# Loads that wait for W_hh, and an output product from fp16 pairs that POOL splits

## The reference, cut to what matters

```python
def _L0_cond_ref(initial_state, inputs, W_ih, W_hh, b_ih, b_hh):   # B 4, T 256, D 256
    def cell(h, x):
        gi = x @ W_ih + b_ih
        gh = h @ W_hh + b_hh
        i_r, i_z, i_n = jnp.split(gi, 3, axis=-1)
        h_r, h_z, h_n = jnp.split(gh, 3, axis=-1)
        r, z = jax.nn.sigmoid(i_r + h_r), jax.nn.sigmoid(i_z + h_z)
        n = jnp.tanh(i_n + r * h_n)
        h_new = (1.0 - z) * n + z * h
        return (h_new, h_new)
...
def _L0_cond2_ref(x, emb, W_emb, b_emb, g_norm, W_qkv, g_q, g_k, W_out):
    scale, shift = jnp.split(emb @ W_emb + b_emb, 2, axis=-1)
    xn = _rms_norm(x, g_norm) * (1.0 + scale) + shift
    q, k, v = ...            # of xn @ W_qkv, 16 heads of 16
    attn = jax.nn.softmax(einsum(_rms_norm(q, g_q), _rms_norm(k, g_k)) * d ** (-0.5))
    o = einsum(attn, v)
    return o + o @ W_out
...
x = x + _L0_attn_ref(_L0_cond_ref(cond_2048, x, ...), ...)
x = x + _L0_ffn_ref(_L0_cond2_ref(x, cond_2048[:, None, :], ...), ...)
```

## Time and profile before

| | us |
|---|---|
| median of 3 runs | 997.29 |
| lowest and highest | 996.51, 998.18 |
| the profiled execution's own time | 998.43 |
| span of its profile | 996.6 |
| PE busy | 937.3 (94% of the span) |
| DVE, ACT, POOL busy | 695.4, 595.1, 582.2 |

### The profile page before, as it was taken

One profiled execution on the slowest core, in us unless ns is written; L12 is line 12 of the kernel. 1 busy time (PEld: TensorE's weight loads), 2 busy tenths in 40 slices (PEclk: granted clock), 3 DMA queues, 4 the chain that ended last, 5 costly groups with the idle time before them and its releaser, 6 DMA issues. The chain is left out here.

```text
span 996.6 us, 37702 instructions
## 1 busy us (share of the span) xinstructions
PE 937.3 (94%) x14997; PEld 755.2 (76%) x14997; DVE 695.4 (70%) x2756; ACT 595.1 (60%) x2053; POOL 582.2 (58%) x1274
## 2 busy tenths in 40 slices
PE   4899999999999999998999999878899999999997
PEld 4889999999999999987888888744455566656564
DVE  6887777777777777776666667778882856656665
ACT  4666666666666666666777777767875432332332
POOL 2577766666666666666677765368302655555652
PEclk7555555555555555557999999999999999999999
DMA  8211111111111011112222231010000143333331
GB/s 345 74 22 18 25 24 25 21 19 25 25 25 24 15 25 25 25 25 86 71 76 87 75 129 41 20 42 1 2 2 1 64 117 129 112 111 122 118 130 44
DMA packets 80474, 58.98 MB, mean 59 GB/s; under 512 B 64918, under 2 KB 71576, under 8 KB 79788
## 3 DMA queue, kind: packets, MB, share of 16 engines
q1 hardware_dynamic: 79108, 56.43, 19.6%
q10 hardware_dynamic: 1192, 0.15, 0.1%
HBM read 47.33 MB, written 8.98 MB: 56 GB/s over the span
## 5 line engine op out<-in xcount | busy, mean ns | idle before, releaser
L589 POOL COPY gp<-hq 128x16 f16<-128x16 f16 x256 | 68.2, 266 | 152.4 <-DVE hq L554 152.4
L2008 PE MATMUL gu<-wq_part 128*128 128x512 f16 x648 | 148.7, 379 | 0.0
L629 POOL TENSOR_TENSOR q_part<-q_raw,q_part 128x64 f16<-128x64 f32 x237 | 112.9, 477 | 19.2
L363 PE MATMUL gq<-gp,wq_part 128*128 128x64 f16 x1422 | 120.6, 242 | 0.0
L287 PE MATMUL gr<-hq,w_one 128*128 128x4 f16 x2048 | 118.7, 166 | 0.0
L347 PE MATMUL gq<-gp,raws 128*128 128x64 f16 x1440 | 115.3, 237 | 0.0
L2008 PEld LDWEIGHTS gu<-wq_part 128*128 128x128 f16 x648 | 63.3, 98 | 65.3 <-issue 0.4
L405 ACT ACTIVATE r_scan<-gr 128x8 f32<-128x8 f32 x256 | 46.6, 182 | 108.8 <-PE gr L287 108.7
L2101 ACT ACTIVATE h_hi<-hT 128x512 f16<-128x512 f32 (+1 forms) x56 | 35.2, 629 | 127.1 <-DVE hT L2178 127.1
L627 POOL CAST q_part<-q_raw 128x64 f16<-128x64 f32 x237 | 110.6, 467 | 0.4
L363 PEld LDWEIGHTS gq<-gp,wq_part 128*128 128x128 f16 x1422 | 94.5, 132 | 0.0
(11 more groups left out here) (305 smaller groups left out, 2764.4 us busy)
## 6 DMA issues: line engine op xcount, KB each, us to landing
wf_ffn<-in_wf SPq DMA_DIRECT2D x28, 384.0 KB, 3.1
kh<-k_kept SPq DMA_DIRECT2D x16, 480.0 KB, 3.6
k_kept<-k_made SPq DMA_DIRECT2D x59, 128.0 KB, 2.8
raw_attn<-in_pairs SPq DMA_DIRECT2D x8, 770.0 KB, 4.6
cw_of<-cw_rows SPq DMA_DIRECT2D x9, 512.0 KB, 3.4
shared<-in_wq SPq DMA_DIRECT2D x1, 2056.0 KB, 13.9
q_part<-in_wk SPq DMA_DIRECT2D x1, 2048.0 KB, 18.0
cw_of<-cw_rows SPq DMA_DIRECT2D x4, 448.0 KB, 3.8
```

What stands on the lines that cost most here:

```text
L363: mm = pe.matmul(q_bank[t % 2][:, 0:B * QB].rearrange("p (b t) -> p b t", b=B), wq_part[:, w, c, j * P:(j + 1) * P], gp[:, g, j, :, h * QB ...
L589: nc.gpsimd.tensor_copy(gp[:, :, :, :, t].rearrange("p q j b -> p q (j b)"), hq[:, nxt, :, 2::3]).then_inc(h_stored, 1)
L629: nc.gpsimd.tensor_tensor(q_part[:, 1, h, :, :, c], src, q_part[:, 0, h, :, :, c], ALU.subtract).then_inc(q_split, 1)
L2008: mm = pe.matmul(dst[:], w[:, c % 2, cols], y[:, j, halves[hf]], start=(n == 0), stop=(n == 3 * J - 1))
```

## The change

At the start: SP waits until the last gate of W_ih has landed before it issues xT, and until W_hh has before it issues Wq; W_emb and its two small companions move ahead of W_k and its bias. The bias rows are made by DVE before the rests of W_ih. The embedding product is spread over eight steps (6 to 13) with one fp32 matmul each; the gain is made in steps 26 and 30. POOL rounds its five heads of Wq in steps 7, 9, 11, 13 and 15.

In the conditioned attention: POOL scales W_out by 64 and splits it into `wo_part`, and splits `oT` of batches 0 to 2 into `o_part` as soon as DVE has copied it; PE's product of these batches is made of 12 fp16 matmuls instead of 4 fp32 ones and waits for that split. The last batch stays fp32 (with the scaled W_out), and DVE's sum divides by 64. POOL's gates are moved behind the next batch's splits.

```diff
-EMB = 9
+EMB = 6
...
             sp.dma_start(whh[:], dram["whh"]).then_inc(loaded["whh"], 16)
+
+            sp.wait_ge(loaded["wih_n"], 16)
             sp.dma_start(xT.rearrange("p j b t -> p j (b t)"), dram["xT"]).then_inc(loaded["xT"], 16)
+            sp.wait_ge(loaded["whh"], 16)
             sp.dma_start(wq, dram["wq"]).then_inc(loaded["wq"], 16)
-            sp.dma_start(bk[:], dram["bk"]).then_inc(loaded["wk"], 16)
-            sp.dma_start(wk, dram["wk"]).then_inc(loaded["wk"], 16)
             sp.dma_start(wemb, dram["wemb"]).then_inc(loaded["emb"], 16)
             sp.dma_start(bemb[:], dram["bemb"]).then_inc(loaded["emb"], 16)
             sp.dma_start(gnorm[:], dram["gnorm"]).then_inc(loaded["emb"], 16)
+            sp.dma_start(bk[:], dram["bk"]).then_inc(loaded["wk"], 16)
+            sp.dma_start(wk, dram["wk"]).then_inc(loaded["wk"], 16)
...
-                if EMB <= t < EMB + 4:
-                    c = t - EMB
-                    if c == 0:
+                if EMB <= t < EMB + 4 * J:
+                    c, j = (t - EMB) // J, (t - EMB) % J
+                    if t == EMB:
                         pe.wait_ge(loaded["emb"], 48)
                         pe.wait_ge(loaded["cond"], 16)
-                    for j in range(J):
-                        mm = pe.matmul(q_bank[0][:, c * B:(c + 1) * B], wemb[:, j, c * P:(c + 1) * P],
-                                       condT[:, j, :], start=(j == 0), stop=(j == J - 1))
-                    if c == 3:
+                    mm = pe.matmul(q_bank[0][:, c * B:(c + 1) * B], wemb[:, j, c * P:(c + 1) * P],
+                                   condT[:, j, :], start=(j == 0), stop=(j == J - 1))
+                    if t == EMB + 4 * J - 1:
                         mm.then_inc(emb_made, 1)
...
-                if EMB + 5 <= t < EMB + 7:
+                if EMB + 4 * J <= t < EMB + 4 * J + 2:
...
-            for g in range(3):
-                cols = gate_cols(g)
-                dve.wait_ge(inputs_one, 2 + g)
-                rest(wih_part[:, 1, :, cols], wih[:, :, cols], WS, wih_part[:, 0, :, cols]).then_inc(inputs_two, 1)
             dve.wait_ge(loaded["bias"], 32)
...
             rest(bias[32:34, :], bias_raw[32:34, :], WS, bias[32:34, :]).then_inc(bias_ready, 1)
+            for g in range(3):
+                cols = gate_cols(g)
+                dve.wait_ge(inputs_one, 2 + g)
+                rest(wih_part[:, 1, :, cols], wih[:, :, cols], WS, wih_part[:, 0, :, cols]).then_inc(inputs_two, 1)
...
-                if t == EMB + 11:
+                if t == EMB + 4 * J + 12:
...
-                if t == EMB + 13:
+                if t == EMB + 4 * J + 16:
...
-                        c = WQ_ACT + h - 2
-                        if 0 <= h - 2 and c < H1:
-                            if h == 2:
+                        c = WQ_ACT + h
+                        if c < H1:
+                            if h == 0:
                                 pool.wait_ge(loaded["wq"], 16)
...
             def batch_product(b):
+
                 free_turn("y", b)
+                pe.wait_ge(out_parts, 5 + 2 * min(b, B - 2))
                 for m in range(J):
-                    for j in range(J):
-                        mm = pe.matmul(turn32[:, m * T:(m + 1) * T], wout[:, j, m * P:(m + 1) * P],
-                                       oT[:, j, batch_cols(b)], start=(j == 0), stop=(j == J - 1))
+                    pairs = [(wo_part[:, w], o_part[:, x]) for w, x in ((0, 0), (0, 1), (1, 0))] if b < B - 1 \
+                        else [(wout, oT[:, :, batch_cols(b)])]
+                    for n, (j, (w, x)) in enumerate(itertools.product(range(J), pairs)):
+                        mm = pe.matmul(turn32[:, m * T:(m + 1) * T], w[:, j, m * P:(m + 1) * P], x[:, j, :],
+                                       start=(n == 0), stop=(n == J * len(pairs) - 1))
                 mm.then_inc(turned, 1)
...
-                            pe.wait_ge(ffn["y_ready"], 4)
+                            pe.wait_ge(ffn["y_ready"], 2)
...
-                nc.vector.tensor_tensor(yT[:, :, batch_cols(b)],
-                                        turn32.rearrange("p (j t) -> p j t", j=J),
-                                        oT[:, :, batch_cols(b)], ALU.add).then_inc(turn_read, 1)
+                nc.vector.scalar_tensor_tensor(out=yT[:, :, batch_cols(b)],
+                                               in0=turn32.rearrange("p (j t) -> p j t", j=J), scalar=1.0 / WQS,
+                                               in1=oT[:, :, batch_cols(b)], op0=ALU.mult,
+                                               op1=ALU.add).then_inc(turn_read, 1)
...
+            flat_wout = wout[:].rearrange("p j n -> p (j n)")
+            nc.gpsimd.tensor_scalar(flat_wout, flat_wout, WQS, 0.0, ALU.mult, ALU.add).then_inc(out_parts, 1)
+            pool.wait_ge(out_parts, 1)
+            nc.gpsimd.tensor_copy(wo_part[:, 0], wout[:]).then_inc(out_parts, 1)
+            pool.wait_ge(out_parts, 2)
+            nc.gpsimd.tensor_tensor(wo_part[:, 1], wout[:], wo_part[:, 0], ALU.subtract).then_inc(out_parts, 1)
...
+            def o_split(b):
+                pool.wait_ge(turn_read, turn_of["out", b] + 1)
+                if b:
+                    pool.wait_ge(turned, turn_of["y", b - 1] + 1)
+                nc.gpsimd.tensor_copy(o_part[:, 0], oT[:, :, batch_cols(b)]).then_inc(out_parts, 1)
+                pool.wait_ge(out_parts, 4 + 2 * b)
+                nc.gpsimd.tensor_tensor(o_part[:, 1], oT[:, :, batch_cols(b)], o_part[:, 0],
+                                        ALU.subtract).then_inc(out_parts, 1)
...
+            o_split(0)
+            y_split(0)
+            o_split(1)
+            y_split(1)
+            gate_of(0)
+            o_split(2)
+            y_split(2)
+            gate_of(1)
+            gate_of(2)
```

More of the change, by code:

```diff
@@ L6 @@
+import itertools
 from contextlib import ExitStack
@@ L437, in _ @@
                     act.wait_ge(loaded["wq"], 16)
-                if EMB + 5 <= t < EMB + 7:
+                if EMB + 4 * J <= t < EMB + 4 * J + 2:
                     act.wait_ge(emb_made, 1)
-                    for c in range(2 * (t - EMB - 5), 2 * (t - EMB - 5) + 2):
+                    for c in range(2 * (t - EMB - 4 * J), 2 * (t - EMB - 4 * J) + 2):
                         nc.scalar.activation(emb[:, c, :], q_bank[0][:, c * B:(c + 1) * B], ACT.Identity,
@@ L1302, in adaln_block @@
         oT = sb("oT2", [P, J, NT])
+        o_part = sb("o_part", [P, 2, J, T], FP16)
+        wo_part = sb("wo_part2", [P, 2, J, D], FP16)
         free_bank = [b[:] for b in ffn["gu_bank"]] + [ctx.enter_context(nc.psum_tensor("cb2", [P, HALF], F32))[:]]
@@ L1326, in adaln_block @@
         y_in, y_temp = sem("y_in"), sem("y_temp")
+        out_parts = sem("out_parts")
         block = ctx.enter_context(nc.Block())
@@ L1835, in _, with y_split @@
             pool.wait_ge(ffn["d_ready"], 1)
-            for b in range(B - 1):
+            raw = temp[:, 0:J * T].rearrange("p (j t) -> p j t", j=J)
+            def o_split(b):
[6 more added lines that the diff above has]
+                                        ALU.subtract).then_inc(out_parts, 1)
+            def y_split(b):
                 cols = batch_cols(b)
-                raw = temp[:, 0:J * T].rearrange("p (j t) -> p j t", j=J)
                 pool.wait_ge(turn_read, turn_of["y", b] + 1)
                 if b:
-                    pool.wait_ge(ffn["y_ready"], 2 * b)
+                    pool.wait_ge(ffn["y_ready"], b)
                 nc.gpsimd.tensor_scalar(x_hi[:, :, cols], yT[:, :, cols], YS, 0.0, ALU.mult, ALU.add)
@@ L1846, in _, with gate_of @@
                                         ALU.subtract).then_inc(ffn["y_ready"], 1)
+            def gate_of(b):
+                cols = batch_cols(b)
                 pool.wait_ge(ffn["lg_read"], b + 1)
```

## The result

The changed kernel takes 999.76 us (median of 14 runs, 997.24 to 1000.92), the kernel before 997.21 us (14 runs beside it, 995.80 to 998.18): a ratio of 1.0023, 95% interval 1.0016 to 1.0029. It is slower by 2.5 us. The forecast was 1.9 us faster, with a range that ended at 997.8, so it was wrong in sign. The profiled execution took 999.79 us, its span is 997.2 us (before: 998.43 and 996.6).

A forecast was written before the change was run, and what follows sets the result against it. Loads and step-to-step waiting bound the scan, PE and DVE waiting on each other the attention, PE the feed-forward. Scan -3.5 and attention +1.6 sum to -1.9 us: median 997.29 to 995.4 us, range 992.8 to 997.8.

The forecast's parts named there:

- part 1: Loads at the start: 1.4 us gained at step 0, 0.4 lost again to W_k, -1.0 us (bounds -1.4 and +0.7).
- parts 2 and 3: Scan: embedding matmuls spread out -1.1 us, POOL's earlier Wq heads -1.1, gain operations moved to later steps -0.3.
- part 4: Attention's output product: +1.1 us each at batches 0 and 1, -0.6 at batch 2, sum +1.6 (bounds -1.8, +2.2).
- The gain at step 0: First scan step: W_hh lands at 9.4 us instead of 10.8 because of the waits, 1.4 us gained.
- The first rival (in-order loads): Start: W_hh still lands at 10.8, part 1 gives 0, total 996.4 us; chance 0.18.
- The bias move: Start, DVE making bias rows ahead of W_ih's rests: through by 9.9 us, so it costs nothing.
- xT itself should land by 12.5: Start: xT, needed by ACT at step 0's end, about 12.8 us, lands by 12.5; no cost given.
- W_k was taken at 24.0: Scan steps 6 and 7: W_k lands at 24.0 us (22.2 to 25.7), losing 0.4 of the 1.4 us.
- W_k late: Rival at scan step 7: W_k at 25.7 us or later, part 1 becomes +0.7, total 997.1 us; chance 0.08.
- The embedding's products: Scan, one fp32 product in each of eight steps: 1.37 us of overrun falls to 0.3, -1.1 us.
- PE's wait on y_ready is lowered to 2: Attention, POOL's splits first and gates after: PE's waits are long met, at no cost.
- The rival in which PE's wait lowers it: Attention: PE's waits halve its clock; one stretch 996.9 us, two 998.8; chance 0.16 (0.10 and 0.06).

The follow-up runs named there:

- e1: Changed kernel with conditioned attention as in the kernel before, so only the start and scan changes: 997.14 us, ratio 1.0003 to the kernel before.
- e2: Changed kernel with attention as before and without SP's two waits (xT behind W_ih_n, Wq behind W_hh): 995.29 us, ratio 0.9986 to the kernel before.
- e8: Changed kernel with attention as before and without xT's wait, Wq's wait behind W_hh kept: 996.34 us, executed once.
- e3: Kernel before with only the change's conditioned attention: 999.04 us, ratio 1.0022 to the kernel before.
- e4: Kernel before with the change's attention, output product behind the next unit's products and DVE's sum behind its maxima: 998.38 us, ratio 1.0014.
- e7: Kernel before with SP's two waits alone (xT behind W_ih_n, Wq behind W_hh): 998.44 us, executed once.
- e9: Changed kernel with POOL's split of y at batches 0 and 1 waiting for DVE's shift rows: 998.59 us, ratio 1.0014 to the kernel before.
- e11: Changed kernel with old attention, no SP waits, old bias order, W_k ahead of the embedding's loads, embedding products from step 7: 995.10 us, ratio 0.9981.
- e12: e11's start, fp16 output product at batch 2 alone, POOL's split of y behind DVE's shift rows at batches 0 and 1: 993.90 us, ratio 0.9967.
- e6: Changed kernel without SP's two waits, with the old bias order and the fp16 output product at batch 2 alone: 995.24 us, ratio 0.9987.
- e10: Kernel before with POOL's split of y at batch 0 waiting for DVE's shift rows: 996.25 us, ratio 0.9992.

## Why the prediction was wrong

**The step that failed is part 1, the loads at the start.** It gave -1.0 us; in the two traces it is +1.97 (-0.69 + 2.66), and between e1 and e2 the waits alone are +1.85. Of the 4.4 us between the forecast's -1.9 and the +2.5 that the four parts sum up to in the traces, part 1 has 3.0, parts 2 and 3 have 0.8 and part 4 has 0.7. Part 1 failed in four places.
- The gain at step 0 was read from one landing time, 10.81, that varies by 1.75 us between executions. That 2.7 us of foreign bytes moved ahead of W_hh was right as arithmetic, but W_hh is there at 9.1 to 9.3 in four of nine kernels without any wait, and on the mean the waits gain nothing. The first rival (in-order loads) had this term right. The Trainium skill's rule that I set against it, "DMA: Bandwidth & Descriptors", section "Queues, rings and completion order", gave 0 for it as well; these runs agree in the number, and don't show in which order the transfers were taken.
- The bias move was put at nothing, because DVE would be through with W_ih's rests by 9.9. It was, at 9.51 (7.62 + 1.89). But PE's input products stand behind these rests, and they keep PE until 12.15. By the 7.99 us from the bias to the state write, W_hh at 9.4 would have brought state write 0 to 13.65 all the same (in e2, with W_hh at 9.29, it stands at 13.61): half of the 1.4 us.
- "xT itself should land by 12.5" was a clause without a price. In the trace of before xT was issued at 3.83 and landed 9.4 us later, at 13.2, so the clause asked for an earlier landing from a later issue. Issued at 7.40, fifteen of its sixteen parts did land by 12.12, but the last came at 15.15, and the reader waits for all. That was 1.0 to 1.7 us at step 1 in three of the four kernels with the wait.
- W_k was taken at 24.0, inside bounds of 22.2 and 25.7. It came at 26.7, beyond the upper one. I priced only the gap ahead of xT, and e8 shows that W_q's wait alone puts W_k at 25.7, against 24.0 in e2. By 12.7 us all queues had moved 2.84 to 3.12 MB in the four kernels with both waits, and 3.43 to 3.71 in those with none. In the changed kernel all queues together had moved 7.42 MB, the loads up to W_k, by 23.5, near the bound's 23.3 (22.1 + 1.2), and the landing then lagged them by 3.2 us, not 2.4. The rival "W_k late" named this and gave it 0.08.

**Parts 2 and 3** were right in direction and too large: -2.0 us on the mean of all profiled executions (nine kernels at 428.27, five at 430.26) for -2.5. No run takes the two parts apart. Step 20 fell from 3.07 to 2.15 us for about 2, as forecast. The embedding's products seem to cost more spread out than 0.3: steps 8 to 19 take 22.35 us in e3 and 21.62 in e2, a gain of 0.7, shared with the earlier heads of W_q, for 1.1.

**Part 4** was right at the product: waits of 1.68 and 1.58 for 1.7, +1.12 at batch 0 (copy to copy) and +1.13 at batch 1 (copy to sum) for +1.1, batch 2 -0.52 for -0.6. The sentence "PE's wait on y_ready is lowered to 2 with POOL's new order ..., and both are long met", at no cost, was wrong by 0.54 us: the order met the semaphores and collided with DVE. Together +2.28 for +1.6.

**The clock.** The rival in which PE's wait lowers it fell: the granted clock is 1.00 from the first copy to the last sum, with PE 1.68 us idle at a time. The Trainium skill, "TensorE: Matmul & The Clock Gate", Part 1, has the gate return to the slow rate after the engine was idle; my strict reading of it, that a PE which is only held up isn't idle, came to the same here. Windows of the changed kernel, then of the kernel before (length, busy time of PE, PEld, DVE, ACT and POOL, granted clock, DMA share, GB/s):

```profile
723.27:772.02 48.75, 42.29 (x448) 24.72 (x445) 25.32 (x58) 31.04 (x63) 13.66 (x18) 1.00 0.01 2
457.21:723.27 266.06, 236.52 (x2481) 191.97 (x2479) 192.46 (x661) 198.26 (x584) 169.97 (x328) 0.99 0.17 55
```

```profile
724.92:771.39 46.47, 43.70 (x436) 25.76 (x433) 24.43 (x58) 30.94 (x63) 8.41 (x12) 1.00 0.01 2
456.96:724.92 267.96, 239.29 (x2481) 193.77 (x2479) 192.35 (x662) 198.75 (x584) 168.10 (x325) 0.98 0.17 55
```

The second line of each is a stretch that the change hardly touches, and it differs by 1.90 us, in favour of the changed kernel. In before the clock rises 6.0 us behind the last state write and falls once more for 3.4 us at 698.5; in after it rises 3.1 us behind it and does not fall. So the profiled pair hides 1.9 of the loss. This is luck of one execution. Part of it goes with the clock: of the 14 profiled kernels six have a second fall between 695 and 704 us (before, e2, e4, e7, e9, e11) and take 266.8 to 268.0 us for this stretch; the eight without it take 266.1 to 266.9. The rest is not explained: e12, at 1.00 throughout, takes 266.5, more than the changed kernel.

Without that stretch the pair differs by +2.5 us (+1.97 - 1.72 + 2.28). That this equals the difference of the medians is in part chance, since 0.56 of the latter lies outside the span. In e1 and e3 by themselves the medians differ by +0.1 and +2.0.

## What to carry to other kernels

A wait put before a load is priced by every load behind it: take each one's own time from issue to landing, add it to the new issue time, and hold it against the moment at which its first reader comes; a transfer with a margin "by eye" gets its number too. A landing time of one execution is a sample, often set by one late part out of sixteen, and a gain that is read from it needs a second trace. When work is reordered on one engine, follow it to the engines that read from it: here DVE was in time and PE was not. Hold the order also against the times of the other engines' operations, not the semaphores alone, as POOL's subtraction and DVE's show. A split on POOL paid here only where PE had other work in the meantime, at batch 2.

## What the runs showed of the hardware that was not expected

- DVE's two-operand subtraction is held while POOL's runs: 0.23 us become 1.23 to 1.24 when POOL's 1.16 us one begins 0.01 to 0.02 us ahead of it (seen in the kernel before, the changed one, e6 and e11), and 0.23 again when POOL is moved away (e9, e10, e12). The profile shows the hold as a longer operation, not as idle time.
- W_hh, 768 KB, is read by ACT at 9.07 to 10.82 us with the same loads issued at the same time; values lie near 9.1 to 9.3 and near 10.5 to 10.8, with one at 9.79. In the four late ones the last one to three of sixteen parts came after 10.2 us, all others by 9.7.
- Holding back the transfers behind it gave 9.70 to 10.35 and no lower mean (10.02 for 9.94), and by 12.7 us 0.3 to 0.9 MB less had moved.
- The scan takes the same time at a granted clock of 0.50 and of 1.00 (428.00 to 428.55, with 428.15 and 428.22 at 1.00).
- The time outside the span was 2.03 to 2.37 us (medians) in the four kernels with the fp16 product at batches 0 and 1, and 1.79 to 1.81 in the others; why is open.
- The granted clock's short fall to 0.50 between 695 and 704 us comes in some executions of a kernel only, and 0.9 us go with it (mean 267.4 for 266.5 us in that stretch).
